# A four-layer graph GRU on one core: in the last layer the state is copied into PSUM beneath the edge sums, two of five low parts of h change engine, and normalisations move ahead of the tanh

## What is computed

```python
for l in range(4):
    m = x @ weight[l]
    agg = segment_sum(m[src], dst)
    gi, gh = agg @ w_ih.T + b_ih, x @ w_hh.T + b_hh
    r, z = sigmoid(i_r + h_r), sigmoid(i_z + h_z)
    n = tanh(i_n + r * h_n)
    x = (1 - z) * n + z * x
return layernorm(node_embed + (x + node_embed))
```

## Time and profile before

| | us |
|---|---|
| median of three runs | 2331.55 |
| the runs | 2330.46 to 2332.36 |
| profiled execution: span from its first to its last instruction | 2327.4 |
| a run's time less that span | 3.1 to 5.0 |
| VectorE busy over the span | 2175.6 (93%) |
| TensorE busy over the span | 2229.5 (96%) |
| ScalarE busy over the span | 1842.3 (79%) |
| GpSimd busy over the span | 1719.4 (74%) |

### The profile page before, as it was taken

How to read it: one execution, slowest core, us unless ns; L and a number is a source line. 1 busy time by engine, 2 the same in 40 slices (tenths; PEclk the granted TensorE clock), 3 DMA queues, 4 the chain that set the end, 5 groups by cost and what they waited for, 6 DMA issues and landing times.

```text
span 2327.4 us, 49180 instructions
## 1 busy us (share of the span) xinstructions
PE 2229.5 (96%) x11728; PEld 1898.3 (82%) x11728; DVE 2175.6 (93%) x4211; ACT 1842.3 (79%) x3483; POOL 1719.4 (74%) x1654
## 2 busy tenths in 40 slices
PE   3999999999999999999999999999989999999996
PEld 2888888888878888888878888888877888888885
DVE  7899999999879999999969999999969999999998
ACT  1688888888768888888857888888856888888886
POOL 3877777777487777777558777777748888888884
PEclk7999999999999999999999999999999999999998
DMA  2455555555545555555545555555544555555554
GB/s 58 120 155 160 158 160 161 158 160 160 157 131 173 171 173 172 174 172 173 166 127 172 172 171 172 173 174 171 174 130 122 159 156 155 155 155 154 155 155 118
DMA packets 277064, 362.45 MB, mean 156 GB/s; under 512 B 107754, under 2 KB 186586, under 8 KB 276980
## 3 DMA queue, kind: packets, MB, share of 16 engines
q1 hardware_dynamic: 238118, 309.12, 43.5%
q0 software_dynamic: 38784, 52.30, 9.7%
q10 hardware_dynamic: 78, 0.08, 0.0%
HBM read 208.71 MB, written 179.20 MB: 167 GB/s over the span
## 4 chain that ended last, share of the span: by engine, by line
PE 66%; DVE 18%; issue 10%; ACT 2%; DMA 2%; POOL 1%; DVEq 1%; SPq 0%; ACTq 0%; POOLq 0%
PE pZ L847 17%; PE pR L847 8%; PE pHN L847 8%; PE pA L835 8%; PE pO L929 5%; PE pIN L847 4%; PE pA L847 4%; DVE bn L1442 3%; PE pR L891 3%; PE pR L888 3%; PE pR L889 3%; DVE diff L1411 3%; DVE aggT L1381 3%; DVE y_rows L1435 2%; PE pH L786 2%
## 5 line engine op out<-in xcount | busy, mean ns | idle before, releaser
L683 POOL DMA_INDIRECT gath<-state,idx x900 | 931.4, 1035 | 264.6 <-issue 255.8
L660 POOL TENSOR_TENSOR h_lo<-hT,h_hi 128x500 fp32r<-128x500 f32 (+1 forms) x400 | 375.8, 940 | 200.5 <-ACT h_hi L1050 149.7
L683 POOL DMA_INDIRECT gath<-in_x_dram,idx x300 | 321.9, 1073 | 101.8 <-issue 68.7
L1080 ACT ACTIVATE rg<-pR,bsum 128x500 f32<-128x500 f32 x400 | 269.7, 674 | 112.2 <-PE pR L891 100.2
L1400 DVE SCALAR_TENSOR_TENSOR narg<-pHN,bhh,rg 128x500 f32<-128x500 f32 x400 | 292.3, 731 | 44.9 <-ACT rg L1080 44.1
L1372 DVE TENSOR_TENSOR a_lo<-aggT,a_hi 128x500 fp32r<-128x500 f32 x396 | 271.5, 686 | 0.3
L1062 ACT CAST sel<-sel 128x504 fp32r (+1 forms) x400 | 245.9, 615 | 31.6 <-DVE flag_i L1356 29.5
L1417 DVE TENSOR_TENSOR diff<-pZ,diff 128x500 f32<-128x500 f32 x400 | 267.7, 669 | 0.8
L1381 DVE TENSOR_TENSOR aggT<-pA,hT 128x500 f32<-128x500 f32 x396 | 263.8, 666 | 1.7 <-PE pA L835 1.6
L1088 ACT ACTIVATE pZ<-pZ,bsum 128x500 f32<-128x500 f32 x400 | 256.1, 640 | 0.0
L1067 ACT CAST a_hi<-aggT 128x500 fp32r<-128x500 f32 x396 | 235.6, 595 | 6.5 <-DVE aggT L1381 6.5
(11 more groups left out here) (211 smaller groups left out, 6384.1 us busy)
## 6 DMA issues: line engine op xcount, KB each, us to landing
columns<-newT SPq DMA_DIRECT2D x300, 250.0 KB, 2.3
hT<-columns SPq DMA_DIRECT2D x300, 250.0 KB, 2.7
state<-o_rows SPq DMA_DIRECT2D x300, 224.0 KB
x_rows<-in_x_dram SPq DMA_DIRECT2D x200, 224.0 KB
out_dram<-o_rows SPq DMA_DIRECT2D x91, 224.0 KB
gath<-state,idx POOLq DMA_INDIRECT x900, 2.4
state<-o_rows SPq DMA_DIRECT2D x297, 26.0 KB
idx<-edge_src SPq DMA_DIRECT2D x395, 1.5 KB
```

What stands on the lines that cost most here:

```text
L660: nc.gpsimd.tensor_tensor(part_of(h_lo, u)[:, cols], hT[:, u % RING, cols], part_of(h_hi, u)[:, cols].bitcast(F32), ALU.subtract).then_inc ...
L683: pool.indirect_dma_start(out=gath[:, u % RING, j, :], out_offset=None, in_=states[l], in_offset=bass.IndirectOffsetOnAxis(ap=idx[:, u % R ...
L1080: nc.scalar.activation(rg[:, :], pR[:, 0:COLS], ACT.Sigmoid, bias=bsum[:, 0:1]).then_inc(s_r, 1)
```

## The change

It touches the last layer only, from its fifth step on (BENEATH is 6, the first block treated in the new way; the last is block 99).

- ScalarE begins each step, ahead of the r gate, with a copy of the state of block b+2 into the sums' bank pA (state_beneath_sums). The copy waits for the low part of the block before it in the bank, block b+1. For block 6 it waits for the aggregate of block 5.
- TensorE's edge sums wait for that copy and add to what is there (start=False).
- VectorE makes no aggT for these blocks. ScalarE's a_hi and VectorE's a_lo read the bank.
- For blocks that leave 1 or 2 when divided by five (block 7, then 11, 12, 16, 17 to 96, 97: 37 in all), VectorE makes the whole of h_lo, after the difference and ahead of the low part of the aggregate, three steps before the block's own, and GpSimd makes none.
- ScalarE's second pair of normalisations moves from behind the z gate to ahead of the tanh.

```diff
--- before.py
+++ after.py
@@ -52,6 +52,8 @@
 PRE = 3
 LATE = 2
 RAMP = 4
+BENEATH = 6
+BY_VECTOR = 1, 2
 UNSPLIT = 10
 AWAKE = 18, 1, 1, 2
 WARMING = 9, 24, 6
@@ -313,6 +315,7 @@
         s_sel8 = sem("selection_bytes_built")
         s_sel = sem("selection_widened")
         s_pA = sem("edges_summed")
+        s_beneath = sem("state_copied_beneath_sums")
         s_agg = sem("agg_made")
         s_R = sem("r_product")
         s_Z = sem("z_product")
@@ -384,6 +387,26 @@
 
             return 0 < l < L - 1
 
+        def beneath(l, i, u):
+
+            return l == L - 1 and not (isinstance(i, int) and i == 0 and u < BENEATH)
+
+        def by_vector(l, i, u):
+
+            return l == L - 1 and u % RING in BY_VECTOR and not (isinstance(i, int) and i == 0 and u < RING + BY_VECTOR[1])
+
+        def low_counts(l, i, u):
+
+            if l < L - 1:
+                return l * NB + UNROLL * i + u + 1, (l - 1) * NB + UNROLL * i + u + 1 if l else None
+            first = sum(by_vector(l, 0, v) for v in range(UNROLL if not (isinstance(i, int) and i == 0) else u + 1))
+            if isinstance(i, int) and i == 0:
+                return l * NB + u + 1 - first, 2 * NB + first if first else None
+            group = sum(by_vector(l, 1, v) for v in range(UNROLL))
+            mine = sum(by_vector(l, 1, v) for v in range(u + 1))
+            return (l * NB + UNROLL - first + (UNROLL - group) * (i - 1) + u + 1 - mine,
+                    2 * NB + first + group * (i - 1) + mine)
+
         def unsplit(l, b):
 
             return l == L - 1 or (isinstance(b, int) and b < UNSPLIT)
@@ -701,7 +724,7 @@
                             for c in range(RING - 1 if l == L - 1 else RING):
                                 gather(l, c, c, 0, True)
                         coming = on_from(l, i, u, PRE)
-                        if coming:
+                        if coming and not by_vector(coming[0], coming[3], coming[2]):
                             split_h(*coming[:3], l * NB + b if exists_before(i, u, 1) else None)
                         half = half_done(i, u, RING + ROWLAG + 1) if l == L - 1 else None
                         if half:
@@ -819,7 +842,12 @@
             def sum_edges(l, b, u, i, start):
                 g = l * NB + b
 
-                at_least(s_agg, g, start)
+                onto = beneath(l, i, u)
+                spreading = l == L - 1 and isinstance(b, int) and b == BENEATH - 1
+                if onto:
+                    pe.wait_ge(s_beneath, UNROLL * i + u - BENEATH + 1)
+                else:
+                    at_least(s_agg, g, start)
                 pe.wait_ge(s_sel, g + 1)
                 if unsplit(l, b):
                     pe.wait_ge(*landed(l, u, turn(i, u)))
@@ -832,7 +860,9 @@
                     pe.wait_ge(s_glo, split_blocks(l, b) + 1)
                 for k, (to, rows, cols, begins) in enumerate(passes):
                     ends = not begins or unsplit(l, b)
-                    last = nc.tensor.matmul(to, rows, cols, start=begins, stop=ends)
+                    if onto or (spreading and k):
+                        begins = False
+                    last = nc.tensor.matmul(to, rows, cols, start=begins, stop=ends, skip_group_check=onto or spreading)
                 last.then_inc(s_pA, 1)
 
             def product(l, u, bank, c, sides, begins=True, ends=True):
@@ -848,12 +878,12 @@
                                             stop=ends and k == len(passes) - 1)
                 return last
 
-            def r_on_state(l, b, u, start, halves, ready=1):
+            def r_on_state(l, b, u, start, by_pool, by_dve=None):
                 g = l * NB + b
-                pe.wait_ge(s_hlo, g + ready)
-                if halves:
-
-                    pe.wait_ge(s_hlov, g + 1 - NB)
+                pe.wait_ge(s_hlo, by_pool)
+                if by_dve is not None:
+
+                    pe.wait_ge(s_hlov, by_dve)
                 at_least(s_r, g, start)
                 product(l, u, pR[:, 0:COLS], 0, ("state",), True, False)
 
@@ -936,7 +966,7 @@
                         b = UNROLL * i + u
                         start = first and l == 0
                         ramp = isinstance(i, int) and i == 0 and u < RAMP
-                        r_on_state(l, b, u, start, halved(l))
+                        r_on_state(l, b, u, start, *low_counts(l, i, u))
                         if not start:
                             hn_on_state(l, b, u, start)
                         if first:
@@ -999,7 +1029,7 @@
                             last = nc.tensor.transpose(pA[:, k * SP:k * SP + ROWS], y_rows[:, 1, k * D:(k + 1) * D],
                                                        ident[0:ROWS, 0:ROWS])
                         last.then_inc(s_pA, 1)
-                        r_on_state(l, b, 0, start, False, PRE + 1)
+                        r_on_state(l, b, 0, start, l * NB + b + PRE + 1)
                         hn_on_state(l, b, 0, start)
                         r_on_sums(l, b, 0)
                         n_on_sums(l, b, 0, None if start else l * NB + b)
@@ -1066,6 +1096,16 @@
                 act.wait_ge(s_pA if summed else s_agg, l * NB + b + 1)
                 nc.scalar.copy(by_rows(a_hi[:, u % RING, :]), sums_of if summed else by_rows(aggT[:, :])).then_inc(s_ahi, 1)
 
+            def state_beneath_sums(l, i, u):
+                b = UNROLL * i + u
+
+                if isinstance(b, int) and b == BENEATH:
+                    act.wait_ge(s_agg, l * NB + b)
+                else:
+                    act.wait_ge(s_alo, l * NB + b)
+                act.wait_ge(s_load[u % RING], 16 * (TURNS * (l - 1) + turn(i, u) + 1))
+                nc.scalar.copy(sums_of, by_rows(hT[:, u % RING, :])).then_inc(s_beneath, 1)
+
             def first_high_part(l, j):
 
                 act.wait_ge(*of_first(j, s_agg0, s_agg, l))
@@ -1151,6 +1191,8 @@
                         ramp = isinstance(i, int) and i == 0 and u < RAMP
                         if not ramp:
                             rows(i, u)
+                        if final and not ramp and exists(i, u, 2):
+                            state_beneath_sums(l, *after(i, u, 2)[:0:-1])
                         r_gate(l, b, u, first and l == 0)
                         if ramp:
                             if u == 3:
@@ -1172,13 +1214,16 @@
                         normal(i, u, 0)
                         if final and not ramp and exists(i, u, 3):
                             widen(l, *after(i, u, 3)[:2])
+                        if not ramp:
+                            normal(i, u, 1)
                         n_gate(l, b, u)
                         if ramp and u < 3:
                             high_part(l, *after(i, u, 1)[:2])
                         if not ramp and exists(i, u, 2):
-                            high_part(l, *after(i, u, 2)[:2])
+                            high_part(l, *after(i, u, 2)[:2], beneath(l, *after(i, u, 2)[:0:-1]))
                         z_gate(l, b, u)
-                        normal(i, u, 1)
+                        if ramp:
+                            normal(i, u, 1)
                         if ramp and u != 1:
                             widen(l, {0: 2, 2: 5, 3: 6}[u], {0: 2, 2: 5, 3: 6}[u])
                         if ramp and u == 3:
@@ -1362,8 +1407,9 @@
 
             def low_h(l, b, u):
                 dve.wait_ge(s_hhi, l * NB + b + 1)
-                v.tensor_tensor(part_of(h_lo, u)[:, HALF:COLS], hT[:, u % RING, HALF:COLS],
-                                part_of(h_hi, u)[:, HALF:COLS].bitcast(F32), ALU.subtract).then_inc(s_hlov, 1)
+                cols = slice(HALF if halved(l) else 0, COLS)
+                v.tensor_tensor(part_of(h_lo, u)[:, cols], hT[:, u % RING, cols],
+                                part_of(h_hi, u)[:, cols].bitcast(F32), ALU.subtract).then_inc(s_hlov, 1)
 
             def low_part(l, b, u, summed=False):
                 dve.wait_ge(s_ahi, l * NB + b + 1)
@@ -1515,7 +1561,8 @@
                         if ramp and u == 3:
                             low_part(l, 4, 4)
                         summed = after(i, u, 1 if ramp else 2)[:2] if exists(i, u, 2) else None
-                        if summed and not (ramp and u == 3):
+                        under = bool(summed) and not ramp and beneath(l, *after(i, u, 2)[:0:-1])
+                        if summed and not (ramp and u == 3) and not under:
                             aggregate(l, *summed)
                         if added and not ramp:
                             remainder(*after(i, u, -ROWLAG))
@@ -1530,11 +1577,11 @@
                         if not opening(i) and exists(i, u, 3) and not final:
                             low_gathered(l, *after(i, u, 3)[:2])
                         coming = on_from(l, i, u, PRE)
-                        coming = coming if coming and halved(coming[0]) else None
+                        coming = coming if coming and (halved(coming[0]) or by_vector(coming[0], coming[3], coming[2])) else None
```

(2 more changed lines are left out.)

## The result

The changed kernel takes 2378.27 us (median of four runs, 2376.93 to 2379.38) against 2331.95 for the kernel before (median of four): a ratio of 1.0199, with a 95% interval from 1.0187 to 1.0212. It is 46 us slower; 45 were forecast.

The account below looks back on a forecast made before the run. VectorE was taken to bound the kernel; after the change a closed loop through ScalarE's copy and r gate, 5.85 us a step against 5.64, would. Its costs, 43.7 + 0.80 + 0.42, make 44.9 on 2331.55: 2376 us, range 2354 to 2390.

Parts of the forecast that it names:

- What bound the kernel: Last layer before the change: VectorE sets the pace, nothing on it waits, a plain step is 5.64 us.
- The lead of ScalarE: Before the change the r gate starts 1.16 us ahead of r times hn, where 0.77 would do; the copy removes it.
- The loop: Last layer, each step: low part, copy, r gate, r times hn, back to low part, 5.85 us against 5.64.
- The low h inside the loop: VectorE's low h stands ahead of the low part, so adds its full 0.59 us in two steps of five.
- remainder 3: Steps whose b leaves 3 when divided by five: a low h makes them 6.44 us against 5.64, +0.80.
- rival B: Low h is free, falling into VectorE's 0.80 us idle time: 22 us less, 2354; chance 0.05.
- Rival C: Low h on VectorE collides with GpSimd, 1.05 us more in each of 37: 39 more, 2415; chance 0.06.
- The normalisations: Moved ahead of the tanh they cost nothing, except remainder 4, where waiting for the shift makes the difference 0.30 us late.
- remainder 4: Steps whose b leaves 4 when divided by five: low h, shift and late tanh, 6.84 us against 5.74, +1.10.
- Edits at nothing: TensorE's sums waiting for the copy (gate possible at 5.31, under 5.85) and GpSimd losing 37 subtractions cost or give nothing.
- The sum: Five steps cost 2.43 us; 18 fives 43.7, step 4 0.80, steps 95 and 96 0.42: together 44.9 us.
- Rival A: Copy finds the low part done, VectorE's shorter work decides: five steps 27.07 from 28.84, 33 us faster, 2298; chance 0.06.

Follow-up runs that it names:

- kernel 9: The kernel before with only the 37 low parts of h moved to VectorE, no copy beneath the sums, normalisations unmoved: 2350.81 us, ratio 1.0088.
- kernel 1: The changed kernel with GpSimd making every low h of the last layer again: 2356.68 us, ratio 1.0109 to the kernel before.
- kernel 2: The changed kernel with VectorE's low h moved behind the product in the last layer: 2354.36 us, ratio 1.0097 to the kernel before.
- Kernel 3: The changed kernel with the second pair of normalisations back behind the z gate: 2373.61 us, ratio 1.0181 to the kernel before.
- kernel 6: Kernel 5 with GpSimd making every low h of the last layer: 2321.52 us, ratio 0.9962 to the kernel before.
- Kernel 4: The changed kernel with ScalarE's copy moved behind the r gate: 2387.68 us, ratio 1.0235 to the kernel before.
- kernel 5: The changed kernel with ScalarE's high part ahead of the tanh, VectorE's low part ahead of the row statistics, normalisations back behind the z gate: 2306.27 us, ratio 0.9892.

## Why the prediction was right, point by point

**What bound the kernel.** Right: VectorE, by kernel 9. The lead of ScalarE, which the trace of before showed, was the cover that the change took away.

**The loop.** Right, with 5.90 measured for 5.85. Its links: low part to copy 0.70 for 0.72, copy to gate 0.52 for 0.49, gate to r times hn 0.78 for 0.77, VectorE's part 3.90 for 3.87. The copy lasts 0.58, as long as the cast less 0.02. The Trainium skill (ScalarE: Activation LUTs, Step-by-step: what each stage is for) says that ScalarE writes PSUM faster than SBUF; the length agrees by those 0.02, but the gate behind it started 0.52 after the copy's start, later than the 0.49 taken, so this link did not get shorter by it.

**The low h inside the loop.** Right: 0.59 in remainder 3 (kernel 1), and nothing when it is moved out (kernel 2), which is rival B made true by an edit. Rival C did not come: the 31 low parts of h in the stretch took 673 ns on average, and of all 37 none took over 0.68 us:

```profile
L1411 DVE TENSOR_TENSOR h_lo<-hT,h_hi 128x500 fp32r<-128x500 f32 x31 | 20.9, 673 | 0.0
```

One low part of the aggregate did take 1.71 us, at 1753.79, ahead of the changed blocks, where it still reads aggT; of the 94 that read the bank none took over 0.68.

**The normalisations.** Right in place, in remainder 4 alone, and a little large: the difference was 0.21 late (2076.83, where the end of the statistics, 2075.83 + 0.87, less the 0.08 by which VectorE starts ahead of the end of what precedes it, would have let it start at 2076.62) for 0.30, mostly because the tanh's result reached VectorE after 0.04, not 0.09. Kernel 3 got 0.24 back.

**Edits at nothing.** Right for TensorE, whose sums still left room: the r product of the plain step ends at 2053.00 (2052.62 + 0.38), so with 0.10 for the handover the gate could come at 2053.10, and it comes at 2053.69. The 0.05 that the prediction took from the copy to the sums is 0.2 in the loop's steps, which does not use up this room. Right for GpSimd at this pace; kernel 6 shows that it holds for this pace only.

**The sum.** 2.43 us in five steps were forecast, 2.62 measured (31.53 - 28.90). Each step came out 0.04 to 0.06 longer than its forecast, since the loop takes 5.90 and not 5.85; against that, the five steps of before are 28.90 and not 28.84. In remainder 4 two errors offset each other, so 6.89 for 6.84 is in part luck: the late tanh cost less than forecast, and the step that closes the loop of ten takes 6.96 where the other takes 6.82 in most passes. Of these 0.14 the copy behind it makes 0.09: as the first instruction of ScalarE's next pass it starts 0.12 after the low part's end (2172.57 + 0.67, then 2173.36), and 0.03 after it in every other step of the loop. The other 0.06 is VectorE's shift, which holds the next instruction 0.16 there (2168.35 to 2168.51) and 0.10 elsewhere; why is not shown. Step 97, which the sum left out, even got shorter, 5.59 for 6.19: it has lost the aggregate, and no copy comes behind it. The parts alone add up: copy 22, low h 21 and normalisations 5 make 48, where 46 were measured. But the low h costs its slot for two reasons: alone because VectorE is full (kernel 9), in the changed kernel because it lies inside the loop (kernels 1 and 2).

**Rival A**, faster by VectorE's relief, needed the gate free of the copy. Kernel 4 shows that the obvious way to free it closes another loop through TensorE, kernel 5 that moving the low part opens both; then the relief comes, 2306, and with the shift moved 2299, near the 2298 of A (31 us under the kernel before beside it, where A had 33). A's reading of VectorE was right; its condition, a gate not held behind the copy, was not met by the changed kernel.

## What to carry to other kernels

When work moves from a full engine to one with room, look at how far the second engine runs ahead: that lead is what hides it, and a copy into a buffer that the first engine has just read takes the lead away, with everything queued behind the copy. Write down the path from the buffer's last reader through the copy and the queue back to that reader, add its lengths, and compare it with the step; if it is longer, the reader has to come earlier in its engine's order, and work that is not on the path belongs behind it. An engine's idle time is only room for what lies outside that path: the same instruction was free on one side of the product and cost its whole length on the other.

## What was not expected of the hardware

How soon TensorE takes up what ScalarE has made depended on where the step stands in the program. In the loop's steps of the changed kernel and of kernel 4 the weight load of the edge sums starts 0.21 to 0.27 after the copy's end in nearly all (0.37 at most); in the written-out steps, but for the first of the changed kernel, it starts 0.05 after it. The last step of the loop and the first behind it, in the changed kernel (the copies end at 2293.09 and 2299.97):

```profile
2292.51 0.58 ACT L1107 COPY pA<-hT 128x500 f32<-128x500 f32 x1 [1.14 <-DVE a_lo L1418]
2293.36 0.87 PEld L865 LDWEIGHTS pA<-sel,gath 128*128 128x128 f32 x6 [1.28 <-issue]
2299.39 0.58 ACT L1107 COPY pA<-hT 128x500 f32<-128x500 f32 x1 [0.88 <-DVE a_lo L1418]
2300.02 0.87 PEld L865 LDWEIGHTS pA<-sel,gath 128*128 128x128 f32 x6 [1.42 <-ACT pA L1107]
```

What stands in between is shown by the view of two lines of the kernel, L851 and L853, at which the sums wait for the selection and for the gathers. Here TensorE's queue (PEldq) runs instructions of its own, ahead of the weight load; the last of these two kinds started at 2293.1 and 2293.3 (count, then shortest, median and longest in ns, then first and last start):

```profile
L851 PEldq ALU_OP  x256: 32/32/36, 128.4 to 2293.1; - x128
L853 PEldq FUSED_REGOPS  x40: 37/42/51, 1795.8 to 2293.3; - x40
```

So the handover from ScalarE to TensorE itself is short, 0.05 us, and the rest goes with these instructions, which the written-out steps at the end do not have. In kernel 4, whose loop runs through the sums, steps of 6.41 to 6.47 against 6.25 to 6.29 show it. No run took the instructions out.

VectorE to ScalarE takes 0.03 to 0.04, but 0.12 where the copy opens a pass of ScalarE's loop. From ScalarE to VectorE it is 0.04 for the difference behind the tanh and 0.11 for r times hn behind the gate. r times hn has two waits, and the chain of the changed kernel shows an instruction of VectorE's queue between the gate's end (2054.36) and its start (2054.47), at the line of one of them; that this makes the 0.07 was not tried.

```profile
2054.39 0.02 DVEq L1445
```
